# Normalised input of the cross-attention turned by transposing transfers instead of TensorE, from the third block on

## The reference, cut to what matters

```python
# x: (4, 2048, 512) f32, ctx_1024: (4, 154, 512); 16 heads of 32; 8 experts, the best 2 of each token
x = x + xattn(layernorm(x), ctx_1024, Wq, bq, Wk, bk, Wv, bv, Wo, bo)
x = x + ffn(layernorm(x), W_experts, b_experts, W_router, b_router)
# xattn: q = h @ Wq.T + bq; k, v from the context; softmax(q k^T / sqrt(32)) v; @ Wo.T + bo
# ffn: softmax of the router's logits, top 2; sum of the two experts' outputs by their weights
```

## Time and profile before

| | |
|---|---|
| median of 3 runs | 1255.27 us (1251.87 to 1256.85) |
| profiled execution: time, span | 1254.02 us, 1252.2 us |
| busy: PE / weight loads | 1172.7 us (94%) / 706.5 us (56%) |
| busy: DVE, POOL, ACT | 869.9 us (69%), 751.4 us (60%), 710.9 us (57%) |
| granted TensorE clock, mean | 0.979 of 2.4 GHz |
| DMA | 239.18 MB, mean 191 GB/s |

### The profile page before, as it was taken

How to read it: one execution, slowest core, us unless ns; L and a number is a source line. 1 busy time by engine, 2 the same in 40 slices (tenths; PEclk the granted TensorE clock), 3 DMA queues, 4 the chain that set the end, 5 groups by cost and what they waited for, 6 DMA issues and landing times. The chain is left out here.

```text
span 1252.2 us, 35422 instructions
## 1 busy us (share of the span) xinstructions
PE 1172.7 (94%) x10864; PEld 706.5 (56%) x10865; DVE 869.9 (69%) x1931; ACT 710.9 (57%) x1040; POOL 751.4 (60%) x996
## 2 busy tenths in 40 slices
PE   8887999999999999999999978699999999999995
PEld 4444666666666666666666645354545555555553
DVE  4766799889889888988987875455545555554553
ACT  4327856966876696697679547243333343333332
POOL 4004446777876877787687678665554555445543
PEclk9979999999999999999999998799999999999998
DMA  9754534865766685577557548779999999998884
GB/s 269 226 156 118 171 118 150 248 185 191 219 207 200 187 253 175 189 231 204 196 157 224 167 139 317 284 183 196 217 190 183 189 184 177 183 172 160 159 161 105
DMA packets 136313, 239.18 MB, mean 191 GB/s; under 512 B 19464, under 2 KB 50184, under 8 KB 135048
## 3 DMA queue, kind: packets, MB, share of 16 engines
q1 hardware_dynamic: 103271, 161.24, 43.0%
q0 software_dynamic: 29808, 67.73, 26.8%
q10 hardware_dynamic: 3120, 8.68, 2.0%
HBM read 112.00 MB, written 101.40 MB: 170 GB/s over the span
## 5 line engine op out<-in xcount | busy, mean ns | idle before, releaser
L1904 PE MATMUL S<-we_s,wq_s 128*128 x1620 | 371.8, 379 | 7.7 <-DVE att L1882 5.7
L1832 POOL DMA_INDIRECT out<-xn,to x135 | 208.9, 1547 | 196.8 <-DMA out<-xn,to 93.4
L1166 POOL TENSOR_TENSOR we_s<-P_s,we_s 128x1024 f16<-128x1024 f32 x96 | 206.6, 2155 | 83.5 <-ACT we_s L932 82.7
L1904 PEld LDWEIGHTS S<-we_s,wq_s 128*128 128x128 f16 x1620 | 156.7, 98 | 172.7 <-issue 11.7
L1843 ACT ACTIVATE wq_s<-PVp 128x512 f16<-128x512 f32 x137 | 81.7, 597 | 261.0 <-PE PVp L1894 247.9
L980 DVE TENSOR_REDUCE mx_sb<-S 128x6 f32<-128x924 f32 x160 | 170.5, 1111 | 11.2 <-PE S L726 10.8
L746 PE MATMUL W<-wo_s,aT_hi 128*128 128x512 f16 x512 | 165.5, 385 | 3.0 <-issue 1.7
L708 PE MATMUL W<-we_s,wq_s 128*128 128x512 f16 x512 | 160.5, 385 | 4.0 <-DVE xnT_lo L958 3.9
L1882 DVE SCALAR_TENSOR_TENSOR att<-S,be_s 128x512 f32<-128x512 f32 x135 | 93.4, 692 | 95.9 <-PE S L1904 90.9
L1262 POOL DMA_INDIRECT dispatched<-xn,idx x112 | 114.9, 1026 | 26.6 <-issue 24.8
L1860 DVE TENSOR_TENSOR wq_s<-PVp,wq_s 128x512 f16<-128x512 f32 x137 | 94.6, 691 | 36.6 <-ACT wq_s L1843 34.1
(11 more groups left out here) (204 smaller groups left out, 1935.1 us busy)
## 6 DMA issues: line engine op xcount, KB each, us to landing
P_s<-dispatched SPq DMA_DIRECT2D x139, 260.5 KB
we_s<-we_s SPq DMA_DIRECT2D x186, 128.0 KB
be_s<-in_x SPq DMA_DIRECT2D x16, 1024.0 KB
xR_s<-in_x SPq DMA_DIRECT2D x16, 1024.0 KB
out<-xR_s SPq DMA_DIRECT2D x16, 1024.0 KB
wst<-in_weT SPq DMA_DIRECT2D x16, 512.0 KB, 5.5
we_scratch<-wsp SPq DMA_DIRECT2D x16, 512.0 KB, 8.9
Kst<-k_scratch SPq DMA_DIRECT2D x16, 480.0 KB, 9.1
```

Source lines behind the costliest of these rows:

```text
L1166: e.tensor_tensor(Pst[1][:, r:r + 2, :], exps(n), Pst[0][:, r:r + 2, :], ALU.subtract).then_inc(pldp, 1)
L1832: e.indirect_dma_start(out, bass.IndirectOffsetOnAxis(ap=to[u][:, :], axis=0), yw[u % YW], None, bounds_check=N - 1, oob_is_err=False, com ...
L1904: m = e.matmul(Yp[:, u % 2, :], gT[u % 2][xp][:, k, :], we_s[:, bass.ds(n * WN + (wp * KC + k) * D, D)], start=(c == 0), stop=(c == 11))
```

## The change

For the first two blocks nothing changes. From the third on (`b.past(2)`), `pe_XT`, `act_XTh` and `dve_XTl` are gone. In their place:

- `act_NX` normalises in place, in `xA`.
- `act_XH` copies each tile of it to f16, into the first half of what was `xn1` (`xh`, ordered by feature group); `pool_XL` on GpSimd subtracts it from the f32 tile into the second half (`xl`).
- `sp_XD` issues two transposing transfers from SyncE, `xh` to `xnT[0]` and `xl` to `xnT[1]`, each 128 x 2048 f16, that is 16 blocks of 128x128. It stands behind the heads' stacking (`sp_RS`) of the block before and ahead of `sp_V`. Ahead of the first it waits for the query matmuls and logits of the block before, which read `xnT`, and for `act_XH`; ahead of the second for `pool_XL`.
- `pe_Q` step 0 and `pe_LA` wait for both transfers (`ld_xT`).
- `sp_XA` of a block waits for the low part of two blocks before, and `act_XH` for the transfers of the block before, since `xh` and `xl` are single.
- ScalarE's third and fourth `act_NX` stand ahead of the row maxima's copy now, with the four `act_XH` behind them; three of the four `pool_XL` stand ahead of the second norm's coefficients, one behind the logits' product.

```diff
@@ -165,6 +165,8 @@
     xR_s = a(nc.sbuf_tensor("xR_s", [P, 2 * NJ * D], F32))
     xR = [xR_s[:, i * NJ * D:(i + 1) * NJ * D].rearrange("p (j d) -> p j d", d=D) for i in range(2)]
     xn1 = a(nc.sbuf_tensor("xn1", [P, NJ, D], F32))
+    xhl = xn1[:, :, :].rearrange("p j d -> p (j d)").bitcast(F16)
+    xh, xl = (xhl[:, i * NJ * D:(i + 1) * NJ * D].rearrange("p (k j n) -> p k j n", j=NJ, n=P) for i in range(2))
     xnT = [carve(KC, TB), a(nc.sbuf_tensor("xnT_lo", [P, KC, TB], F16))]
     qs = [carve(NG, TB) for _ in range(2)]
     Qst = [carve(H, TB) for _ in range(2)]
@@ -284,6 +286,7 @@
     nrs = [s_(f"nrs{i}") for i in range(2)]
     nap = [s_(f"nap{i}") for i in range(2)]
     t1p, t1h, t1e = s_("t1p"), s_("t1h"), s_("t1e")
+    t1l, ld_xT = s_("t1l"), s_("ld_xT")
     qp, qhe, qle = s_("qp"), s_("qhe"), s_("qle")
     mxp, mxr, mtp, mte = s_("mxp"), s_("mxr"), s_("mtp"), s_("mte")
     stp, exd, phd, pldp, pldd = s_("stp"), s_("exd"), s_("phd"), s_("pldp"), s_("pldd")
@@ -621,9 +624,42 @@
                      bias=nrm[n][:, 6, j:j + 1]).then_inc(nap[n], 1)
 
     def act_NX(e, b, j):
-        if j == 0 and b.past(1):
+        if j == 0 and b.past(1) and not b.past(2):
             e.wait_ge(t1p, b.at(4))
-        act_apply(e, 0, b, j, xA[b.par], xn1)
+        act_apply(e, 0, b, j, xA[b.par], xA[b.par] if b.past(2) else xn1)
+
+    def act_XH(e, b, j):
+        if j == 0 and b.past(3):
+            e.wait_ge(ld_xT, b.at(32, -64))
+        elif j == 0:
+            e.wait_ge(t1p, 4 * 2)
+        e.wait_ge(nap[0], b.at(NJ, j + 1))
+        e.activation(xh[:, :, j, :], xA[b.par][:, j, :].rearrange("p (k n) -> p k n", n=P), ACT.Copy).then_inc(t1h, 1)
+
+    def pool_XL(e, b, j):
+        e.wait_ge(t1h, b.at(4, j + 1))
+        e.tensor_tensor(xl[:, :, j, :], xA[b.par][:, j, :].rearrange("p (k n) -> p k n", n=P), xh[:, :, j, :], ALU.subtract).then_inc(t1l, 1)
+
+    def sp_XD(e, b):
+        e.wait_ge(qp, b.at(4))
+        hold(e)
+        e.wait_ge(lap, b.at(1))
+        hold(e)
+        e.wait_ge(t1h, b.at(4, 4))
+        hold(e)
+        turned(e, 0, xh)
+        e.wait_ge(t1l, b.at(4, -4))
+        hold(e)
+        turned(e, 1, xl)
+
+    def turned(e, part, src):
+        e.dma_start_transpose(xnT[part].rearrange("p k (j n) -> p (k j) n", n=P), src.rearrange("p k j n -> p (k j n)")).then_inc(ld_xT, 16)
+
+    def wait_turned(e, b):
+        if b.past(2):
+            e.wait_ge(ld_xT, b.at(32, -32))
+        else:
+            e.wait_ge(t1e, b.at(4, 4))
 
     def act_NY(e, b, j):
         if j == 0:
@@ -659,6 +695,8 @@
         for back in range(1, len(chain) + 1):
             name, off = chain[at - back]
             b = s + (off - (back > at))
+            if name.startswith("XT") and b.past(2):
+                continue
             if b.here():
                 kind = name.rstrip("0123456789")
                 signal, n = EMPTIED[kind]
@@ -698,7 +736,7 @@
             pe_value(e, 2)
             e.wait_ge(p_bk, 5)
         if i == 0:
-            e.wait_ge(t1e, b.at(4, 4))
+            wait_turned(e, b)
         if part == 0:
             if free := emptied(f"Q{i}", s):
                 e.wait_ge(*free)
@@ -902,6 +940,7 @@
             e.wait_ge(restack[(NB - 1) % 2], 192 * NB // 2)
             e.wait_ge(stp, 10 * (NB - 1))
             e.wait_ge(nap[0], NJ * NB)
+            e.wait_ge(t1l, 4 * (NB - 2))
             load_experts(e, 0, 3)
             e.dma_start(be_s[:, :], be.rearrange("(a e) n -> a (e n)", a=1).broadcast_to([P, NE * D])).then_inc(ld_ew, 16)
         e.wait_ge(stp, b.at(10, n + 1))
@@ -1280,7 +1319,10 @@
         return src[bass.ds(b.at(TB), TB), :].rearrange("(j p) d -> p j d", p=P)
 
     def sp_XA(e, b):
-        if b.past(2):
+        if b.past(4):
+            e.wait_ge(t1l, b.at(4, -12))
+            hold(e)
+        elif b.past(2):
             e.wait_ge(nap[0], b.at(NJ, -NJ))
             hold(e)
         e.dma_start(xA[b.par][:, :, :], blk_rows(x, b)).then_inc(ld_xA[b.par], 16)
@@ -1397,7 +1439,7 @@
             pe_ST(e, b, 5, s)
             pe_PV(e, b, 0)
             pe_PV(e, b, 1)
-        if on_bp2:
+        if on_bp2 and not bp2.past(2):
             pe_XT(e, bp2, 0, s)
         if on_bm1:
             pe_O(e, bm1, 0, s)
@@ -1554,13 +1596,15 @@
             act_WEh(e, bp2)
         if on_bp3:
             act_NX(e, bp3, 1)
+            act_NX(e, bp3, 2)
+            act_NX(e, bp3, 3)
+        if on_bp3 and bp3.past(2):
+            for j in range(NJ):
+                act_XH(e, bp3, j)
         if on_bp1:
             act_MTe(e, bp1)
         if on_bm1 and not bm1.last:
             act_norm(e, 1, bm1)
-        if on_bp3:
-            act_NX(e, bp3, 2)
-            act_NX(e, bp3, 3)
         if on_bp2:
             act_Qh(e, bp2, 2)
         if on_bp1:
@@ -1610,7 +1654,7 @@
             dve_ATl(e, bm2, 3)
         if on_bm1:
             dve_PL(e, bm1, 4)
-        if on_bp1:
+        if on_bp1 and not bp1.past(2):
             dve_XTl(e, bp1, 0)
         if on_bm1:
             dve_NM(e, bm1, 0)
@@ -1710,9 +1754,14 @@
             pool_BX(e, b, 3)
         if early1:
             pool_S1(e, bm1, 2)
+        if on_bp4 and bp4.past(2):
+            for j in range(NJ - 1):
+                pool_XL(e, bp4, j)
         if on_b and not b.last:
             pool_NC(e, b, 1)
             pool_RQ(e, b)
+        if on_bp4 and bp4.past(2):
+            pool_XL(e, bp4, NJ - 1)
         if early1:
             pool_S1(e, bm1, 3)
         elif on_bm1 and bm1.here(NB - 3):
@@ -1727,7 +1776,11 @@
             sp_XR(e, bm2)
         if on_b:
             sp_K(e, b)
+        if on_b:
             sp_RS(e, b)
+        if on_bp1 and bp1.past(2):
+            sp_XD(e, bp1)
+        if on_b:
             sp_V(e, b)
         if on_bp1:
             sp_WL(e, bp1)
@@ -2007,7 +2060,7 @@
             act_prepare(e)
             slots(e, act_slot, -2, 3)
             e.wait_ge(qp, 4 * NB)
-            e.wait_ge(t1p, 4 * NB)
+            e.wait_ge(ld_xT, 32 * (NB - 2))
             act_hi(e, 0, 0)
             act_hi(e, 0, 1)
             act_hi(e, 0, 2)
```

## The result

| | before | after |
|---|---|---|
| median | 1255.2 us | 1291.4 us (1287.6 to 1297.3, 4 runs) |
| ratio, 95% interval | | 1.0296 (1.0246 to 1.0346) |
| span of the profiled execution | 1252.2 us | 1292.6 us |
| busy PE, DVE, POOL, ACT | 94, 69, 60, 57% | 90, 66, 64, 56% |

The forecast was 1284 us, with a range of 1232 to 1345.

What follows compares the result with a forecast made beforehand. It took PE's own queue to bound the attention slots, 44.05 us each. Waits net of saved transposes (+17) and half-clock stretches (+12) made +29 us on 1254.0, 1284 in terms of the median; range 1232 to 1345.

Steps and rivals of the forecast that it cites:

- PE loses 1.88 us of transposes a slot: On PE, 16 transposes of the normalised input go in each of 14 blocks, all on the bound: 26.3 us gained.
- L: On SyncE's queue, time from the first transposing transfer's issue until both have landed: taken as 8.2 us, 5.1 of it free.
- the wait: At a slot's first query matmul PE waits 3.1 us for the transfers; net +1.2 us a slot, +17 in 14.
- The clock, +12: PE's clock halves for 3.4 us after such a wait, costing 1.7 us, in half the slots: +12 us.
- GpSimd's subtractions: Four added on GpSimd, 1.1 us each, three ahead of the second norm's coefficients; could cap the gain at 20 us.
- The sum of +29 us: Whole kernel: +17 us from waits net of the removed transposes, and +12 us from the clock, giving 1284 us.
- ScalarE's copies, 0: Four f16 copies at the slot's end, 2.2 us, fit with two normalising steps into ScalarE's 6.29 us wait: cost 0.
- Rival A: The transfers are hidden, L at most 5.1 us: 1229 to 1235 us; chance 0.27 including partial gains.
- Rival B: The transposing goes by small pieces, L 13.5 us or more, PE waits 8.4 a slot: 1370 us; chance 0.17.

Runs made afterwards that it cites:

- the control: The kernel before with only `dve_WEl` moved, to the place it has in the other runs that move it: 1267.8 us (1.0070 to 1.0138).

## Why the prediction came out right, and where it did not

The sign and the size came true: 1291 against 1284. By its steps:

- **PE loses 1.88 us of transposes a slot: right in the work, wrong in the worth.** "So in these slots PE's own queue is the bound, and what is taken out of it shortens a slot" fails. Without any transfer, and with `dve_WEl` out of its long collision, a slot took 44.5 us instead of 42.2. The condition behind it, "as long as nothing else is due later", was not met: a second loop was as long as PE's queue (the control), and of 1.88 us some 0.6 could be had, by estimate. A trace of it in before was DVE's wait of 0.2 us a slot for GpSimd's bias addition, which I had not read.
- **L and the wait: right in kind, the wait a third too large.** Predicted 8.2 and 3.1 us (43 us in all); 9.4 in the slot shown, and 2.3 us of waiting on average (31.6 us in 14 slots), because PE arrived later than I had it (6.7 us after the first issue, not 5.1). What the step did not have is that 5.8 of the 9.4 us are the queue's issuing of two transposing transfers.
- **The clock, +12: mis-sized.** It fell behind the transfer wait in 5 of the 14 slots (and behind the two collisions) and not in 7, which at 1.7 us each is 8 us of matmuls; filling the waits gave 1.5 us net, up to 7 by the estimate above.
- **GpSimd's subtractions, "cap the gain at 1.44 us a slot": the step that failed.** I followed their delay on GpSimd to the next idle time and stopped. It reached DVE through lgq, and there met `dve_WEl`: 24 us with the transfers out of the way, 5 in the change itself (1291.4 - 1286.7). The prediction had named the place to look ("GpSimd's coefficients"), without a price. Its cap of 1.44 can't be redone from the two idle times that it names: 3.62 + 1.66 less 4.4 us of subtractions leave 0.9.
- **The sum of +29 us came near the +36 partly by luck.** Roughly, as estimates, the terms came as 32 us of waits, up to 8 of clock and 5 of collision, less the 10 that the transposes could give: 35. The waits were put 12 us and the clock 4 us too high, which made up for a gain put 16 us too high and a collision that was not in the sum.
- **ScalarE's copies, 0: nothing speaks against it.** They take 0.62 us each (0.55 predicted), and PE's waits for ScalarE in the slots are the same few in both kernels, 1.1 us at most. No run tested it alone.
- **Rival A (1229 to 1235)** did not come, since L was above 5.1; and its times would not have come with L below 5.1 either: with the transfers ahead of the stacking no wait for them was left, and the time was 1280, 1256 with `dve_WEl` moved. In the queue a transposing transfer is not as cheap as a plain one, 2.8 to 3.3 us against 0.5. The Trainium skill (Advanced Engine Details and Errata, section X-Bar Transpose) calls the two equally fast and says nothing of the issue. For the time behind the second issue the first such slot agrees (4.6 us and 4.7); for the issue, and so for how long PE waits, the measurement decides.
- **Rival B (1370)** did not come: pieces under 512 B rose from 19464 to 77703 packets, and L was 9.4, not 13.5.

## What to carry to other kernels

Before counting work taken from the busiest engine as gained, test whether a second loop is as long as its queue: one deliberate delay of 1 us on GpSimd in the kernel before would have shown it. Small waits that recur in every slot, here 0.2 us of DVE for GpSimd, say where to try; they prove nothing, since DVE waited longer elsewhere (1.4 us a slot, for GpSimd's part of the logits). When work moves to GpSimd, list the DVE instructions with two SBUF inputs near the time to which its instructions shift, and check each for a meeting; moving one out of a collision needs the same check at its new place, with a control on the kernel before. Where two causes hold the same slot, remove each with and without the other, since either alone can look nearly free. And a mean clock of 1.00 over 400 us does not say that the clock never fell: look right behind the waits.

## What the hardware showed unexpectedly

- A DVE instruction with two SBUF inputs and a GpSimd instruction at the same time ran one after the other here, in either order: 1.21 us became 3.56 (DVE behind GpSimd), 0.39 became 1.44 (GpSimd behind DVE), and a run of four small DVE instructions took 4.57 us in place of 0.64, behind two of GpSimd in a row.
- A transposing transfer of 512 KB from SBUF to SBUF held SyncE's queue for 2.8 to 3.3 us in the median, a plain one of the same bytes for 0.54. Behind the issue they landed alike in the one slot that can be compared.
- The clock did not fall behind every wait of PE: in the change it was 0.54 behind one of 2.71 us and 1.00 behind one of 2.51; with `dve_WEl` moved it was 0.52 behind one of 3.34 us, 0.51 behind one of 2.41 and 1.00 behind one of 2.57.
